# The first feed-forward layer with the weights held in TensorE and the tokens moving

## What is computed

```python
pooled = x.mean(axis=1)                                   # x is normed, (8, 112, 256)
probs = softmax(tanh(pooled @ W1 + b1) @ W2 + b2)         # 8 zones
top_p, top_i = top_k(probs, 3)                            # 3 zones for each batch
top_w = top_p / top_p.sum(axis=-1, keepdims=True)
for e in top_i:                                           # Wa: (8, 256, 1024), Wb: (8, 1024, 256)
    zone_outputs += (gelu(x @ Wa[e]) @ Wb[e]) * w[e]
x = x + tanh(g_ffn) * (x + zone_outputs)
```

## Time and profile before

| | |
|---|---|
| median of 3 runs | 465.81 us (462.35 to 468.35) |
| span of the profiled execution | 464.4 us |
| PE busy | 434.6 us (94%) |
| DVE, ACT, POOL busy | 241.8 us, 202.5 us, 140.6 us |
| L1143, first layer | 288 matmuls, 71.5 us |
| L1155, transposes | 192, 27.0 us |
| L1169, second layer | 576 matmuls, 67.1 us |
| granted TensorE clock, mean | 0.974 |

### The profile page before, as it was taken

One profiled execution on the slowest core, in us unless ns is written; L12 is line 12 of the kernel. 1 busy time (PEld: TensorE's weight loads), 2 busy tenths in 40 slices (PEclk: granted clock), 3 DMA queues, 4 the chain that ended last, 5 costly groups with the idle time before them and its releaser, 6 DMA issues. The chain is left out here.

```text
span 464.4 us, 9442 instructions
## 1 busy us (share of the span) xinstructions
PE 434.6 (94%) x2832; PEld 322.2 (69%) x2833; DVE 241.8 (52%) x483; ACT 202.5 (44%) x467; POOL 140.6 (30%) x128
## 2 busy tenths in 40 slices
PE   0869999999999999999999999979999999999996
PEld 0527677676777766777777777648777788877885
DVE  2534546776876876876886875543222212222222
ACT  1122554454555544545545554535443343443332
POOL 5351246356355445454445446200000000000000
PEclk9955999999999999999999999989999999999999
DMA  6480562643733633734734632110101001010000
GB/s 203 84 217 29 125 164 90 162 148 103 176 118 110 181 105 108 177 110 109 183 103 115 159 89 79 42 29 21 31 1 32 10 19 30 1 30 25 5 11 12
DMA packets 33910, 41.19 MB, mean 89 GB/s; under 512 B 12502, under 2 KB 28174, under 8 KB 33886
## 3 DMA queue, kind: packets, MB, share of 16 engines
q1 hardware_dynamic: 27678, 23.25, 20.0%
q0 software_dynamic: 4832, 17.11, 12.1%
q10 hardware_dynamic: 1376, 0.53, 0.5%
HBM read 33.22 MB, written 7.66 MB: 88 GB/s over the span
## 5 line engine op out<-in xcount | busy, mean ns | idle before, releaser
L635 DVE TENSOR_REDUCE negmax<-bank 112x1 f32<-112x375 f32 x128 | 68.5, 547 | 44.4 <-PE bank L955 41.1
L484 ACT ACTIVATE probs<-bank,negmax 112x375 f32<-112x375 f32 x128 | 72.5, 571 | 43.2 <-DVE negmax L635 43.1
L979 PE MATMUL bank<-pT,vpad 125*32 125x112 f32 x768 | 86.9, 263 | 2.3 <-issue 1.0
L492 ACT ACTIVATE pT<-bank 125x672 f32<-125x672 f32 x64 | 46.7, 730 | 83.0 <-PE bank L964 82.6
L899 DVE SCALAR_TENSOR_TENSOR stage<-bank,wcur,stage 128x448 f16<-128x448 f32 x48 | 32.7, 684 | 95.2 <-ACT stage L589 95.1
L979 PEld LDWEIGHTS bank<-pT,vpad 125*32 125x32 f32 x768 | 71.2, 111 | 14.2 <-issue 6.2
L1143 PE MATMUL bank<-wa,ctxT 128*112 x288 | 71.5, 385 | 1.7 <-DMA ctxT<-x_scr 1.7
L1169 PE MATMUL bank<-wb,stage 128*112 x576 | 67.1, 273 | 1.4 <-DVE stage L899 1.4
L1169 PEld LDWEIGHTS bank<-wb,stage 128*112 128x112 f16 x576 | 63.6, 130 | 5.3 <-issue 1.8
L964 PE MATMUL bank<-ident,probs 112*125 112x112 f32 x384 | 59.4, 292 | 0.0
L589 ACT ACTIVATE stage<-bank,wcur 128x448 f16<-128x448 f32 x48 | 30.2, 630 | 59.3 <-PE bank L1155 47.6
(11 more groups left out here) (96 smaller groups left out, 405.7 us busy)
## 6 DMA issues: line engine op xcount, KB each, us to landing
stage<-in_L_ffn_Wa POOLq DMA_DIRECT2D x16, 512.0 KB, 4.7
stage<-in_L_ffn_Wb POOLq DMA_DIRECT2D x16, 512.0 KB, 4.4
ctx_s<-in_ctx SPq DMA_DIRECT2D x8, 375.0 KB
k_scr<-k_hl SPq DMA_DIRECT2D x16, 187.5 KB
kst<-k_scr SPq DMA_DIRECT2D x8, 375.0 KB, 5.2
kst<-k_scr SPq DMA_DIRECT2D x16, 187.5 KB, 3.6
q_scr<-q_hl SPq DMA_DIRECT2D x16, 112.0 KB
qst<-q_scr SPq DMA_DIRECT2D x8, 224.0 KB, 4.2
```

The lines of the kernel that those rows point to most:

```text
L484: a.activation(probs[:, p % 2, e, :], bank[0:SQ, 2 * (p % 2) + e, 0:SK], ACT.Exp, bias=negmax[:, h:h + 1], accum_out=rowsum[:, par, h:h + ...
L492: a.activation(pT[:, p % 2, :, :], flat[0:CK, PTB:PTB + KC * 256].rearrange("p (c f) -> p c f", c=KC)[:, :, 0:2 * SQ], ACT.Copy).then_inc( ...
L635: v.tensor_reduce(negmax[:, h:h + 1], bank[0:SQ, 2 * (p % 2) + e, 0:SK], AX.X, ALU.max, negate=True).then_inc(s["dve_max"], 1)
L979: ins = T.matmul(o, vpad[:, c, p, 32 * e:32 * e + 32], pT[:, p % 2, c, e * SQ:(e + 1) * SQ], start=(e == 0 and c == 0), stop=(e == 1 and c ...
```

## The change

The first layer's operands change places: a 128 by 128 block of `wa` is stationary and the 112 tokens move. The result of a half is four blocks of 128 features by 112 tokens, 448 columns in bank 0 or 1, already transposed. So `ht`, `ht_hi` and the semaphore `ht_full` go. `gelu` writes 128 by 448 into `h_f`; DVE multiplies by the share for the high part (a new `tensor_scalar`) and makes the low part with both inputs in SBUF instead of one in PSUM. `hT` becomes two buffers, both in `kst` behind `h_f`, taken in turn, so that the product for a unit waits for the second layer of two units ago.

```diff
         h_f = kflat[:, 0:2 * FT * SQ].bitcast(F32)
-        hT = stage[:].rearrange("p a f -> p (a f)")[:, 0:2 * FT * SQ].bitcast(F16)
+        hT = [kflat[:, (1 + i) * 2 * FT * SQ:(2 + i) * 2 * FT * SQ] for i in range(2)]
...
-                act.wait_ge(s["g1_done"], u_done * 2 + hf + 1)
-                act.wait_ge(s["ht_full"], u_done * 2)
-                a.activation(h_f[:, hf * 512:(hf + 1) * 512], bank[0:SQ, hf, :], ACT.Gelu_apprx_tanh,
+                act.wait_ge(s["g1_done"], u * 2 + hf + 1)
+                if not (isinstance(u, int) and u == 0):
+                    act.wait_ge(s["htlo_done"], u * 2 - 1 + hf)
+                a.activation(h_f[:, hf * 448:(hf + 1) * 448], bank[:, hf, 0:448], ACT.Gelu_apprx_tanh,
                              scale=1.0 / WSCALE).then_inc(s["gelu_done"], 1)
...
-                a.activation(hT[:, hf * 448:hf * 448 + 448], bank[:, 2 + hf, 0:448], ACT.Copy,
-                             scale=wcur[:, par, k:k + 1]).then_inc(s["hthi_done"], 1)
...
+                        dve.wait_ge(s["gelu_done"], u * 2 + hf + 1)
+                        if hf == 0 and not (isinstance(u, int) and u < 2):
+                            dve.wait_ge(s["g2_done"], u - 1)
+                        v.tensor_scalar(hi, h, wcur[:, par, k:k + 1], None, ALU.mult).then_inc(s["hthi_done"], 1)
                         dve.wait_ge(s["hthi_done"], u * 2 + hf + 1)
...
-                        ins = T.matmul(o, x2b[:, par, xs * DT * SQ + t * SQ:xs * DT * SQ + (t + 1) * SQ],
-                                       wa[:, bass.ds(e * (4 * CHUNK) + ws * (2 * CHUNK) + t * CHUNK + hf * 512, 512)],
...
+                for f in range(4):
+                    o = bank[:, hf, f * SQ:(f + 1) * SQ]
+                    n = 0
+                    for t in range(DT):
+                        for ws, xs in ((0, 0), (0, 1), (1, 0)):
+                            ins = T.matmul(o, wa[:, bass.ds(e * (4 * CHUNK) + ws * (2 * CHUNK) + t * CHUNK + hf * 512 + f * 128, 128)],
+                                           x2b[:, par, xs * DT * SQ + t * SQ:xs * DT * SQ + (t + 1) * SQ],
...
-                    ht(b, k, 0)
                     if nxt:
                         g1(*nxt, 0)
-                    ht(b, k, 1)
-                    if nxt:
                         g1(*nxt, 1)
```

More of the change, by code:

```diff
@@ L573, in _, with gelu @@
             act.wait_ge(s["lo_done"], NCH)
-            def gelu(u_done, hf):
-                act.wait_ge(s["g1_done"], u_done * 2 + hf + 1)
-                act.wait_ge(s["ht_full"], u_done * 2)
-                a.activation(h_f[:, hf * 512:(hf + 1) * 512], bank[0:SQ, hf, :], ACT.Gelu_apprx_tanh,
-                             scale=1.0 / WSCALE).then_inc(s["gelu_done"], 1)
[L582 to L588, removed]
-                a.activation(hT[:, hf * 448:hf * 448 + 448], bank[:, 2 + hf, 0:448], ACT.Copy,
-                             scale=wcur[:, par, k:k + 1]).then_inc(s["hthi_done"], 1)
+            def gelu(u, hf):
+                act.wait_ge(s["g1_done"], u * 2 + hf + 1)
+                if not (isinstance(u, int) and u == 0):
+                    act.wait_ge(s["htlo_done"], u * 2 - 1 + hf)
+                a.activation(h_f[:, hf * 448:(hf + 1) * 448], bank[:, hf, 0:448], ACT.Gelu_apprx_tanh,
+                             scale=1.0 / WSCALE).then_inc(s["gelu_done"], 1)
             def ffn_body(b, par, last):
@@ L596, in ffn_body @@
                         route_hidden(1)
[L597 to L600, removed]
+                    if not (last and k == TOPK - 1):
+                        gelu(n + 1, 0)
+                        gelu(n + 1, 1)
                     if isinstance(b, int) and b == 0:
@@ L1138, in g1 @@
                     pe.wait_ge(s["gelu_done"], u * 2 - 1 + hf)
-                o = bank[0:SQ, hf, :]
-                n = 0
-                for t in range(DT):
-                    for xs, ws in ((0, 0), (0, 1), (1, 0)):
-                        ins = T.matmul(o, x2b[:, par, xs * DT * SQ + t * SQ:xs * DT * SQ + (t + 1) * SQ],
-                                       wa[:, bass.ds(e * (4 * CHUNK) + ws * (2 * CHUNK) + t * CHUNK + hf * 512, 512)],
-                                       start=(n == 0), stop=(n == 3 * DT - 1))
-                        n += 1
-                ins.then_inc(s["g1_done"], 1)
[L1149 to L1153, removed]
-                for f in range(4):
-                    ins = T.transpose(bank[:, 2 + hf, f * SQ:(f + 1) * SQ], h_f[:, hf * 512 + f * 128:hf * 512 + (f + 1) * 128],
-                                      ident[0:SQ, 0:SQ])
-                ins.then_inc(s["ht_full"], 1)
+                for f in range(4):
[5 more added lines that the diff above has]
+                                           x2b[:, par, xs * DT * SQ + t * SQ:xs * DT * SQ + (t + 1) * SQ],
+                                           start=(n == 0), stop=(n == 3 * DT - 1))
+                            n += 1
+                ins.then_inc(s["g1_done"], 1)
             def g2(b, par, k, e):
@@ L1168, in g2 @@
                     for hs, ws in ((0, 0), (0, 1), (1, 0)):
[L1169 removed]
+                        ins = T.matmul(o, hT[(par + k) % 2][:, hs * FT * SQ + f * SQ:hs * FT * SQ + (f + 1) * SQ],
                                        wb[:, bass.ds(e * (4 * CHUNK) + ws * (2 * CHUNK) + f * D, D)],
```

13 lines of the change are left out of this document (8 added, 5 removed).

## The result

The changed kernel takes 489.16 us (median of 4 runs, 487.36 to 491.11) against 464.4 us (median of 4, 462.35 to 468.35) for the kernel before: the ratio is 1.0515, 95% interval 1.0474 to 1.0555. It is slower, as forecast, and 10.6 us above the forecast of 478.6: inside the stated range of 465 to 492, but above the 472 to 487 that the forecast had for itself. The profiled execution (491.11 us, the slowest of the four) has a span of 489.4 us, 25.0 more than before, where the forecast had 12.8 more. Medians are over all executions of a kernel, while ratios leave out two that ran in a slower state of the chip, one of them (496.27 us) of the kernel with one hT buffer.

The account below looks back on a forecast made before the run. TensorE's sequencer, working out run-time weight addresses, was to bound the kernel at 7.02 us a unit against 6.29: loop +13.1, ahead of it nothing, end -0.3, together +12.8 on the span, so 478.6 us, 2.7% slower; range 465 to 492.

Parts of the forecast that it names:

- The rival of a cheaper step: TensorE's sequencer: address steps cost between 0.100 and 0.120 us, time stays within 2%, middle 467 us; chance 0.10.
- the faster case: Feed-forward units: PE, not its sequencer, is the limit at 5.31 us a unit, 443 us in all; chance 0.12.
- One of its marks: Sign of being right, first layer: PE idle in short pieces before its matmuls, ended by "issue".
- loads and matmuls one behind the other: Rival, first layer: pairs in series at 100 ns, 7.42 us of PE a unit, 488 us; chance 0.08.
- The step price: TensorE's sequencer: 0.124 us for each run-time weight address, 0.11 where the step is an ALU_OP.
- The pair of load and matmul: First layer on PE: a 128-column weight load with its 112-column matmul takes 56 ns, 48 pairs 2.69 us a unit.
- Zone 0.80, once a unit: TensorE's sequencer: fetching the run-time zone number takes 0.80 us, counted once in each unit.
- Wait values 0.37: TensorE's sequencer: working out values to wait for, mean 3.7 instructions at 0.1, 0.37 us a unit.
- the jump 0.05: The loop's jump on TensorE's sequencer: 0.05 us a unit, the loop's mean 6.29 less a steady unit's 6.24.
- Ahead of the loop: nothing: Unit-by-unit code before the loop: 24.9 us against 24.92 before, so no change.
- The end: -0.3: Last units after the loop: 16.6 us against 16.91, as a wait of 1.14 for ACT and DVE goes.
- 0.6 us of slack: Batch's end: VectorE's chain takes 6.0 us, the second layer asks after 6.6, so it delays nothing.

Follow-up runs that it names:

- the run with the zone handed on: Changed kernel keeping the zone's number for the second layer in 4 of the 8 places where it is fetched twice; 484.79 us, ratio 1.0446 to the kernel before.
- the first experiment: Changed kernel with the 32 run-time first-layer addresses of a unit replaced by fixed ones (zone 0's weights); 436.91 us, ratio 0.9406 to the kernel before.

## Why the prediction was right, and where it was too small

**The bound.** Right. The unit is set by the sequencer's steps: fixed addresses take 52 us away, 8 steps fewer take 0.129 us each, and a fetch added is a fetch paid. The rival of a cheaper step is out (0.124 us with PE empty, as with PE behind), and with it the faster case, which needed just that. That PE alone would be faster is right as well: 4.98 us a unit where 5.31 was forecast. One of its marks hardly showed: PE has no row running in only 7.4 of the loop's 134 us, since a matmul's row lasts 218 ns and the next begins 87 ns later; the waits are to be seen in the distance between starts.

**The time, and some luck.** The time itself doesn't bear the mechanism out. It lies above the forecast's own 472 to 487, in the part of the range that was kept for loads and matmuls one behind the other: that rival had 488 us and 7.42 us a unit, and measured were 489.16 and 7.44. Only the runs with fixed and with fewer addresses tell the two apart (49 ns a pair). That the total came inside the range although two terms of the sum were too small was luck.

**The step price and the first layer: too small by 4%.** 32 x 0.124 = 3.97 were forecast; over the loop the first layer's steps take 4.13 us a unit in the starts of the sequencer's rows, and the second layer's 16 take 1.92 where 1.83 was forecast. The price was read from six even steps, and one step in eight is longer. That is 18 x (0.16 + 0.09) = 4.5 of the 7.6 us by which the loop exceeded its forecast (20.7 instead of 13.1). The pair of load and matmul was taken at 56 ns between 47 and 111; it is 49. It plays no part in the changed kernel's time, as the prediction said.

**Zone 0.80, once a unit: the step that failed.** The price was about right: with the step that works out the place of the number, a fetch takes 0.75 us in the loop's rows (0.67 more a unit where one was added; 0.86 less where one was taken away, with the cheaper steps behind it). The count was not: 24 fetches in 18 units, not 18. They take 17.9 us where 18 x 0.80 = 14.4 were forecast, 3.5 of the 7.6. In the kernel before they were there as well, hidden under TensorE; a mean over steady units could not show them, a count over the whole loop would have.

**Wait values 0.37 and the jump 0.05.** Both about right: 0.34 and 0.07 us a unit in the same rows, together 0.2 us less in the loop than forecast. Writing out the loop took 5.53/18 = 0.31 a unit; each of the two jumps back costs 0.7 to 0.95 us.

**Ahead of the loop: nothing; measured +2.4.** One second fetch, 0.9 by the run with the zone handed on (27.28 - 26.41, the stretch read in the same way there). The longer steps again: the four first layers take 17.0 us of steps where 4.5 + 3 x 3.97 = 16.4 were forecast, the three second layers 5.9 instead of 5.5. The rest, some 0.5, was not settled. In the forecast TensorE had no wait here; the profile shows one and names ScalarE (timeline of the kernel after, and line 1127 in the window 312 to 313):

```profile
312.88 4.32 PE L1141 MATMUL bank<-ctxT,wa 128*128 128x112 f16 x48 [0.57 <-ACT kst L580]
```

```profile
L1127 PEldq TENSOR_LOAD <-idx_row x1: 313/313/313, 312.1 to 312.1; - x1
```

The first gelu was done at 312.36; the fetch of the next zone's number, begun at 312.12, holds the first address until 312.78, so this too is the sequencer.

**The end: -0.3; measured +0.4.** The wait of 1.14 went, as forecast, and taking the second buffer away brought it back at 1.41. A second fetch stands here too, with VectorE's name on it again (timeline of the kernel after):

```profile
474.11 2.84 PE L1157 MATMUL bank<-wb,kst 128*112 x24 [0.69 <-DVE kst L896]
```

**VectorE at a batch's end.** The prediction gave it 0.6 us of slack and held, although the trace of the changed kernel names VectorE at these very places: the mark that it had set down as proof against it ("idle before the second layer that ends with DVE") did appear and meant something else. The 6.0 us that it had summed up for VectorE are 355.04 to 361.10, 6.06, in the batch start shown above, and the sequencer's first layer ends at 361.98. Handing on the zone made these waits go without touching VectorE.

**The second buffer: nothing more.** Right in the loop; 1.4 us once at the end.

**The sum.** +12.8 was forecast, +25.0 measured on the span. Of the 12.2 between them 1.5 are taken for scatter ahead of the stage, 7.6 lie in the loop, 2.4 ahead of it and 0.7 at the end. Of the loop's 7.6, 4.5 are longer steps and 3.5 the six second fetches, less 0.2 to 0.4 for the values to wait for and the jump.

## What to carry to other kernels

A matmul whose operand address is known only at run time has a price on TensorE's sequencer that doesn't depend on its size, here 0.124 us an address (0.129 in the mean); a change that cuts the matmuls finer multiplies it, so count addresses per unit beside columns, and count fetches over the whole loop, not over one clean unit. If the choice can be made once, by a copy of the chosen block into a fixed place on an engine with time to spare, the fine cut becomes the gain that it looked like: 438 us instead of 489. And where the chain of waits names an engine and then shows a stretch of "issue" behind it, look at the sequencer's rows in that stretch before believing the name.

## What the runs showed of the hardware that was not expected

- A load of 128 columns of 16-bit weights is faster than one of 112: 98 against 130 ns, as the rows of the first experiment show (min/median/max):

```profile
L1141 PEld LDWEIGHTS bank<-ctxT,wa x1152: 95/98/152, 305.5 to 426.3; 128*128 128x128 f16 x192
...
L1157 PEld LDWEIGHTS bank<-wb,kst x576: 126/130/132, 312.0 to 431.5; 128*112 128x112 f16 x192
```

  The Trainium skill's page "TensorE: Matmul & The Clock Gate" ("Weight-path perf modes") says that a faster load is used only with all 128 columns and outside 32 bit; these two rows agree in sign. Neither length shows in the time of a unit here.
- VectorE copies 4096 columns of 16 bit in 1.227 us, 0.30 ns a column, where its product from 32 to 16 bit takes 451 ns for 448, 1.0 a column. The Trainium skill's page "VectorE: DVE Perf Modes" ("What auto-detection actually checks") names 16 bit on both sides with step 1, one source and both in SBUF as what its fastest mode needs; that is this copy, and the row agrees.
- The fetch of one number into TensorE's sequencer is worth five to seven address steps, in the kernel after 0.67 to 0.86 us in the open.
- The address step doesn't follow TensorE's clock: between 308.2 and 310.9 us of the kernel after the granted clock was 0.50 (1.2 of 2.4 GHz), and the steps there are 0.124 us apart as at 1.00.
